# Two-layer cross-attention kernel: the opening's plan is reordered, two x tiles are normalised on VectorE, and the context's second half is split quarter by quarter

## The reference, cut to what matters

```python
q = (query @ Wq).reshape(b, t, h, d)          # query: layernorm(x)
k = (key @ Wk).reshape(b, t, kv_h, d)         # key, value: ctx_4096
v = (value @ Wv).reshape(b, t, kv_h, d)
q = apply_rope(q)                             # x * cos + rotate_half(x) * sin
k = apply_rope(k)
```

## Time and profile before

| what | us |
|---|---|
| median of 3 runs (849.8 to 850.12) | 849.99 |
| the profiled execution's own time | 849.6 |
| its span | 847.8 |
| TensorE busy in the span | 836.6 |
| VectorE, ScalarE, GpSimd busy | 521.2, 372.3, 351.2 |

### The profile page before, as it was taken

How to read it: one execution, slowest core, us unless ns; L and a number is a source line. 1 busy time by engine, 2 the same in 40 slices (tenths; PEclk the granted TensorE clock), 3 DMA queues, 4 the chain that set the end, 5 groups by cost and what they waited for, 6 DMA issues and landing times.

```text
span 847.8 us, 12558 instructions
## 1 busy us (share of the span) xinstructions
PE 836.6 (99%) x4706; PEld 695.6 (82%) x4706; DVE 521.2 (61%) x994; ACT 372.3 (44%) x927; POOL 351.2 (41%) x275
## 2 busy tenths in 40 slices
PE   7999999999999999999999999999999999999998
PEld 6878888888888888888877778898888888888877
DVE  6856655655555655655666537555366667677784
ACT  6443123223122222222223143467797877787752
POOL 4777534644544644543545440112232431233442
PEclk9999999999999999999999999999999999999999
DMA  8122311411311410310311122011010200300002
GB/s 303 51 64 73 89 38 32 119 39 28 97 38 27 124 39 25 100 40 19 103 42 40 53 83 82 13 39 50 14 38 26 57 31 14 125 14 1 1 1 99
DMA packets 25036, 48.15 MB, mean 57 GB/s; under 512 B 3600, under 2 KB 5008, under 8 KB 24848
## 3 DMA queue, kind: packets, MB, share of 16 engines
q1 hardware_dynamic: 24544, 47.22, 18.6%
q10 hardware_dynamic: 432, 0.14, 0.1%
HBM read 45.12 MB, written 2.23 MB: 56 GB/s over the span
## 4 chain that ended last, share of the span: by engine, by line
PE 92%; DVE 2%; POOL 2%; ACT 2%; issue 1%; DMA 1%; SPq 0%; POOLq 0%
PE PB L1261 23%; PE PB L1263 23%; PE PB L1262 23%; PE PB L1420 8%; PE PB L1351 4%; PE PB L1325 3%; PE PB L1435 3%; PE PB L1268 3%; PE PB L1335 1%; PE PB L1372 1%; DMA xs<-in_x 1%; POOL qb L807 1%; DVE st L1066 1%; ACT Eb L904 0%; PE PB L1386 0%
## 5 line engine op out<-in xcount | busy, mean ns | idle before, releaser
L807 POOL TENSOR_TENSOR qb<-qb,arena 128x512 f32<-128x512 f32 x64 | 83.7, 1308 | 151.3 <-DVE arena L1123 151.3
L1045 DVE TENSOR_TENSOR xs<-xs,PB 128x512 f32<-128x512 f32 x111 | 75.6, 686 | 96.9 <-PE PB L1263 88.9
L876 ACT ACTIVATE Oh<-PB 96x128 fp32r<-96x128 f32 (+2 forms) x236 | 79.4, 360 | 56.0 <-PE PB L1351 36.7
L1261 PE MATMUL PB<-WOh,Oh 128*128 128x512 f32 x242 | 94.5, 390 | 0.0
L1263 PE MATMUL PB<-WOh,Ol 128*128 128x512 f32 x242 | 94.2, 389 | 0.0
L1262 PE MATMUL PB<-WOl,Oh 128*128 128x512 f32 x242 | 94.2, 389 | 0.0
L1120 DVE TENSOR_TENSOR qb<-PB,ropeq 128x512 f32<-128x512 f32 x64 | 44.2, 691 | 69.4 <-PE PB L1263 68.4
L876 ACT ACTIVATE WOh<-stage 128x512 fp32r<-128x512 f32 (+1 forms) x32 | 19.5, 620 | 132.6 <-PE PB L1263 132.6
L1261 PE MATMUL PB<-xTh,WQh 128*128 128x512 f32 x192 | 76.5, 399 | 0.0
L784 POOL TENSOR_TENSOR WOl<-stage,WOh 128x512 fp32r<-128x512 f32 (+1 forms) x32 | 40.5, 1277 | 84.2 <-ACT WOh L876 70.3
L784 POOL TENSOR_TENSOR WQl<-stage,WQh 128x512 fp32r<-128x512 f32 x38 | 48.9, 1290 | 62.6 <-ACT WQh L876 61.9
(11 more groups left out here) (242 smaller groups left out, 2174.9 us busy)
## 6 DMA issues: line engine op xcount, KB each, us to landing
stage<-in_wq SPq DMA_DIRECT2D x44, 256.0 KB, 2.8
stage<-in_wo SPq DMA_DIRECT2D x44, 256.0 KB, 2.7
arena<-recs SPq DMA_DIRECT2D x32, 256.0 KB, 3.9
stage<-in_wk SPq DMA_DIRECT2D x13, 256.0 KB, 2.7
arena<-in_ctxT SPq DMA_DIRECT2D x8, 256.0 KB, 5.0
stage<-in_wv SPq DMA_DIRECT2D x8, 256.0 KB, 3.9
xs<-in_x SPq DMA_DIRECT2D x8, 256.0 KB, 6.0
out<-xs SPq DMA_DIRECT2D x7, 256.0 KB, 2.0
```

The costliest lines, as they stand in the source:

```text
L807: e.tensor_tensor(dst, dst, tmp, ALU.add).then_inc(s_radd)
L876: return e.activation(dst, src, ACT.Copy)
L1045: e.tensor_tensor(xs[:, i, :], xs[:, i, :], PB[b][:, :], ALU.add).then_inc(free[b])
L1261: e.matmul(dst, Ah, Bh, start=(k == 0), stop=False)
```

## The change

The arithmetic stays the same. What moves:

- The mask, the rotary tables and the identity become one input `tab` (128 x 272), loaded by SyncE behind the first `wq0` weight; ScalarE issues no DMA any more. The second half of the context and of x is loaded ahead of the second `wq0` weight, and `wk0_load` goes ahead of x tiles 2 and 3.
- A step `warm`: ten 128x128 matmuls of the ones that GpSimd has just written, into bank 5. Nothing reads them.
- `k0(0, 0)` starts on the first high parts (`hi x hi`, then `lo x hi`, then `hi x cTl`), chunk by chunk. `v0_first` makes three v0 tiles at once, all products with `WVh` first, those with `WVl` behind.
- `k0(1, 0)` goes ahead of the transposes. The rope of a key or query tile is a step of its own (`rope`), so VectorE and GpSimd can run it elsewhere than TensorE computes the tile.
- Tiles 1 and 3 are normalised by VectorE (`xn_v`), 0 and 2 by ScalarE.
- `ctx 1` (the context's second half) is four steps spread between others. `k0(0, 1)` goes ahead of the queries.
- The mask's work is two steps, `keep` and `many`; `many` has a bank of the ring and stands behind `q0(0, 0)`.

```diff
-    split("wk0", 0)
-    step("mask_tables")
-    step("ctx", 0)
-    for c in range(2):
-        split("wv0", 0, c)
+    step("tab_load")
     step("ctx_load", 1)
     for i in HI:
         step("x", i)
+    split("wk0", 0)
+    for c in range(4):
+        step("ctx", 0, c)
+    for c in range(2):
+        split("wv0", 0, c)
+    step("wk0_split")
+    split("wq0", 0)
...
     stage("k0", 0, 0)
+
     for i in range(3):
-        stage("v0", 0, i)
-    step("wk0_split")
+        tile("v0", 0, i)
+    step("v0_first")
+    stage("k0", 1, 0)
+    step("ctx", 1, 0)
     step("v0_move", 0, 0)
-    split("wq0", 0)
+    step("ctx", 1, 1)
+
+    step("xn", 0, 0)
+    step("xn_v", 0, 1)
+    step("ctx", 1, 2)
+    step("rope", "k0", 0, 0)
+    for i in range(2):
+        stage("xT", 0, i)
+    step("xn", 0, 2)
+    step("xn_v", 0, 3)
+    for i in range(2):
+        step("xsplit", 0, i)
+    step("ctx", 1, 3)
+    stage("xT", 0, 2)
+    step("xsplit", 0, 2)
     step("v0_move", 0, 1)
-    normed(0, LO, [None, lambda: stage("v0", 0, 3)])
+    stage("v0", 0, 3)
+    stage("xT", 0, 3)
+    step("xsplit", 0, 3)
+    step("rope", "k0", 1, 0)
     for i in range(2, 4):
         step("v0_move", 0, i)
+    stage("k0", 0, 1)
     for i in range(1, 4):
         split("wq0", i)
-    step("ctx", 1)
+    step("keep")
     for i in HI:
         step("stats", 0, i)
     step("rstd", 0, 4)
-    stage("k0", 1, 0)
-    for n in range(4):
+    step("rope", "k0", 0, 1)
+    stage("q0", 0, 0)
+    stage("many")
+    step("rope", "q0", 0, 0)
+    for n in range(1, 4):
         q0(0, n)
-    stage("k0", 0, 1)
```

```diff
+                elif kind == "warm":
+                    pe.wait_ge(s_one, 1)
+                    for _ in range(10):
+                        e.matmul(PB[5][:, 0:128], pTb[:, 0, 0:128], pTb[:, 0, 0:128], start=True, stop=True)
...
+                elif kind == "xn_v":
+                    ph, i = k
+                    dve.wait_ge(s_ln, 12)
+                    if eb_users(ph, i):
+                        dve.wait_ge(*done(*eb_users(ph, i)))
+                    e.tensor_scalar(Eb[:, i % 2, :], xs[:, i, :], lnb[:, 1, i:i + 1], lnb[:, 4, i:i + 1], ALU.mult,
+                                    ALU.add).then_inc(s_xnv)
```

## The result

| | before | changed |
|---|---|---|
| median of 9 runs each, us | 849.8 | 852.1 |
| lowest to highest | 849.41 to 850.8 | 851.56 to 853.08 |
| ratio, 95% interval | | 1.0025, 1.0016 to 1.0034 |
| span of the profiled execution | 847.8 | 849.8 |
| start of `b0(0)` in it | 44.20 | 46.31 |

A forecast was written before the change was run, and what follows sets the result against it. TensorE was taken as the bound, so the change counts by `b0(0)`'s start: the opening's gains are outweighed by ScalarE's queue and VectorE's table wait, moving it from 44.20 to 46.35, +2.15 us on 849.99: 852.1, range 851.2 to 853.0.

The forecast's parts named there:

- VectorE's rope for the tables: Before `v0(0, 7)`: first query rope waits for GpSimd's tables, last rope ends at 44.2, `b0(0)` +2.15 us; chance 0.52.
- Landings 0.54 us earlier: At the start: ScalarE's three small transfers leave the front, so all that follows in the queue lands 0.54 us earlier.
- xn_v 0.35 us, ceiling 0.69: VectorE's normalising beside `k0(1, 0)`: 0.35 us taken, 0.69 at most; cost on the path nothing, at the ceiling 0.3.
- The tables 3.5 us: VectorE before the first query rope: 3.5 us for GpSimd's addition and tables, of which `many` covers 0.25.
- Who holds the transposes: Third and fourth transposes wait behind ScalarE's queue of 3.3 us; the fourth starts at 20.1.
- its own bound of 17.7: Before the third transpose: the rope freeing bank 0 ends by 17.7 at most, while ScalarE's third `Eb` comes at 17.4.
- TensorE stands some 3 us: From the transposes to `k0(0, 1)`: TensorE waits some 3 us, to 21.7; without any wait over at 19.4.
- the low clock in the opening: Rival, chance 0.20: low level holds through `k0(0, 0)`, 1.1 us later, 853.2; if it rises only at 12, 854.0.
- The prediction's chance of a slower kernel, 0.68: Whole kernel: slower, beginning at 851.7 us, was given 0.68, same 0.20, faster 0.12.
- The covered tables: Rival, chance 0.16: VectorE's wait for the tables is absent or covered; `v0(0, 7)` at 41.15, -1.0 us, 849.0.
- TensorE as the bound throughout: Rival, chance 0.12: waits for ScalarE and tables both vanish; `b0(0)` at 40.9, -3.3 us, 846.7.

The follow-up runs named there:

- the best version: The changed kernel with tables early, copies of v0 tiles 1 and 2 early, all four tiles normalised by ScalarE, rope of `k0(1, 0)` moved up: 848.2 us, ratio 0.9982.

## Why the prediction was right, and where its terms were off

Forecast 852.1 us, measured 852.1. The mechanism was the one named: VectorE's rope for the tables, the last rope at 44.2 (44.18 measured), `v0(0, 7)` at 44.3 (44.24), `b0(0)` at 46.35 (46.31), and nothing behind. The run with the tables early took that away and got the 2.1 us back. But three terms were mis-sized: the first two made the chain 0.9 us too short, the third made it 0.9 us too long. That the sum came out to the tenth is luck.

- **Landings 0.54 us earlier.** The step "I put all that follows in the queue 0.54 us earlier" failed. The last x stats began at 12.34, where 11.7 was forecast and 12.07 stood before; rstd ended at 15.63 instead of the forecast 14.9, `v0_first` began at 9.59 instead of the forecast 9.15. The table put at the front again moved the median by 0.16 us only. 432 packets' share of the engines' time is no delay of the chunks; what sets that varies from run to run.
- **xn_v 0.35 us, ceiling 0.69.** It was 1.62 and 0.61, and 0.55 alone. The nearest row by tile size said nothing of the neighbour, and the ceiling was no bound. Between them, landings and `xn_v` put `k0(0, 1)` at 22.84 instead of 21.7 and VectorE's rope of it at 33.09 instead of 32.2.
- **The tables 3.5 us.** It was 2.62 from the rope's end (33.09) to the first query rope (35.71). `ropeq` took 0.46 us and `many` 0.24; before, they took 0.91 and 0.56. Before, they ran while VectorE computed `cTl`; now VectorE stands still and waits for them. That this is the reason isn't shown by a run of its own. This 0.9 us cancelled the 0.9 us before it.
- **Who holds the transposes.** The prediction had ScalarE's queue for the third and fourth. The third waited 1.34 us for VectorE's rope (L1158), the case that its own bound of 17.7 should have excluded; that rope ended at 18.61 + 0.68 = 19.29, since rstd came 0.7 later and `xn_v` took 1.3 more. The fourth didn't wait at all: it started at 21.28 one step behind the last matmul of `v0(0, 3)`, and the copy that frees its bank was over at 20.92. The 0.96 us before `k0(0, 1)` was for the copy as said. "TensorE stands some 3 us" doesn't follow from the prediction's own times, 21.7 less 19.4 being 2.3; the two waits came to 2.30.

Of the rivals: the low clock in the opening didn't come, `k0(0, 0)` went in steps of 0.23 with waits between. Its price was overrated as well: 1.1 us was forecast for the low level through `k0(0, 0)`, and the run without the ones, at that level to 8.9, lost nothing measurable. The prediction's chance of a slower kernel, 0.68, is a little more than its parts give (0.52 less a fifth to a tenth, plus 0.20: 0.62 to 0.67). The covered tables (849.0) is what the run with them early shows: there 849.99, since `k0(0, 1)` starts at 22.76 and not at 21.7. TensorE as the bound throughout (846.7) was never reached; the best version came to 848.2 with `b0(0)` at 42.62 instead of 40.9. A falling clock behind a wait late in the opening was among no rivals.

## What to carry to other kernels

Before moving a step behind another, follow each of its parts through every engine: the mask's few tables cost 2.1 us, with an addition on GpSimd ahead of them and four ropes on VectorE behind them. An engine made faster at the start gives nothing while its banks come free no sooner: the ones showed nothing in two kernels, the early copies nothing on top of the early tables, and the ones were worth 1.4 us once the other waits were gone. And when forecast terms are added, bound each by rows that have the same neighbour on the other engines, not only the same tile.

## What the hardware did that was not expected

- A float32 tensor_scalar of 128x512 on VectorE, SBUF to SBUF: 0.55 us alone, 0.90 and 0.61 with GpSimd's subtraction already running, 1.62 when it began within 0.04 us. Each of the three that overlap ends 0.28 or 0.29 us behind the end of one of GpSimd's operations (17.29 behind 17.00, 19.94 behind 19.65, 19.17 behind 18.89), and the GpSimd operation that follows takes 1.47 to 1.49 us instead of 1.27 to 1.30. By the Trainium skill (SBUF — State Buffer, "SBUF: two separate sides") VectorE in a 2-port mode and GpSimd take the same port pair as an exclusive lock, for a whole instruction. The trace agrees with the blocking, though by its start times VectorE was first in the longest of them and still ended last.
- GpSimd's small table operations: 0.46 and 0.24 us with VectorE idle, 0.46 and 0.25 beside the tiny operations of `rstd` (tables early), 0.91 and 0.56 in the kernel before, beside a subtraction on VectorE. The first reads another tile there (`rope`, not `tab`), so the neighbour isn't the only difference.
- TensorE's granted clock fell to 0.50 from 46 to 48 us behind waits of 0.17 and 1.47 us in one version, and stayed at 1.00 when six unread matmuls filled the second. The changed kernel, with the same wait of 1.47 us in its trace, had a mean clock of 1.000 in eight of nine runs.
- ScalarE could take the second 256 KB chunk of the context at 5.13 us in one profiled execution and at 7.90 in another. Up to 6.6 us this didn't move `v0_first` by more than 0.5 us where the ones ran; at 7.27 and 7.90 the start of `b0(0)` moved with it.
